# Four-layer decoder on one core: score and value matmuls of a batch issued together in the two 16-head cross-attention stages

## The reference

```
q = x_n @ w_q                  # 4 x 256 x (16 x 64)
k, v = context @ w_k, context @ w_v   # 4 x 512 x (16 x 64)
p = softmax(q k^T / 8)         # per head: 256 x 512
x = x + (p v) @ w_out + b_out
```

## Time and profile before

| | |
|---|---|
| runs shown | 2795.58, 2800.47, 2803.43 us |
| profiled execution | 2792.92 us, span 2791.1 us, mean granted PE clock 0.941 |
| PE busy | 2510.5 us, 90% of the span |
| PE weight loads | 1594.0 us, 57% |
| DVE busy | 1776.8 us, 64% |
| ACT busy | 1530.3 us, 55% |
| POOL busy | 1364.9 us, 49% |
| L918, scores matmuls | 768 instructions, 190.3 us |
| L945, flips of layer 0's cross stage | 512 instructions, median 273 ns |
| L968, value matmuls | 1280 instructions, 167.0 us |

### The profile page before, as it was taken

One profiled execution on the slowest core, in us unless ns is written; L12 is line 12 of the kernel. 1 busy time (PEld: TensorE's weight loads), 2 busy tenths in 40 slices (PEclk: granted clock), 3 DMA queues, 4 the chain that ended last, 5 costly groups with the idle time before them and its releaser, 6 DMA issues. The chain is left out here.

```text
span 2791.1 us, 57927 instructions
## 1 busy us (share of the span) xinstructions
PE 2510.5 (90%) x20585; PEld 1594.0 (57%) x20585; DVE 1776.8 (64%) x4074; ACT 1530.3 (55%) x4979; POOL 1364.9 (49%) x1981
## 2 busy tenths in 40 slices
PE   6899978988989988978559999789999999999997
PEld 3555544645655655646444555446666666666665
DVE  4566655545656755555554555478887888778884
ACT  2455544622756755633224555357667776777664
POOL 0344443400536642420003444388878878788873
PEclk8899998998998999999777999899999999999998
DMA  2000000000000010000010000101011011101000
GB/s 72 1 1 1 1 9 1 10 27 14 2 5 1 2 34 1 1 6 1 8 29 1 1 1 1 52 20 36 24 32 35 24 36 32 36 24 43 25 22 11
DMA packets 45711, 47.85 MB, mean 17 GB/s; under 512 B 11947, under 2 KB 31413, under 8 KB 45430
## 3 DMA queue, kind: packets, MB, share of 16 engines
q1 hardware_dynamic: 45430, 44.18, 5.7%
HBM read 31.05 MB, written 0.52 MB: 11 GB/s over the span
## 5 line engine op out<-in xcount | busy, mean ns | idle before, releaser
L1033 DVE TENSOR_REDUCE negmax<-scores 128x1 f32<-128x508 f32 (+4 forms) x512 | 212.5, 467 | 212.4 <-PE scores L918 181.1
L1013 POOL TENSOR_TENSOR l_xattn_probs<-l_xattn_probs,rowinv 128x512 f32<-128x512 f32 x128 | 130.4, 1040 | 421.1 <-DVE rowinv L1025 421.1
L2277 ACT ACTIVATE net_probs<-bank,net_negmax 128x96 f32<-128x96 f32 x768 | 251.6, 340 | 112.0 <-DVE net_negmax L2413 111.0
L1013 POOL TENSOR_TENSOR lora_probs<-lora_probs,rowinv 128x508 f32<-128x508 f32 (+1 forms) x256 | 149.6, 618 | 245.0 <-DVE rowinv L1025 245.0
L2331 POOL TENSOR_TENSOR net_rope<-net_rope,net_sin_parts 128x512 f32<-128x512 f32 x192 | 244.5, 1273 | 10.4 <-DVE net_sin_parts L2383 10.4
L2339 POOL TENSOR_TENSOR net_probs<-net_probs,net_inverse 128x384 f32<-128x384 f32 x192 | 158.8, 827 | 119.7 <-DVE net_inverse L2409 118.0
L2352 POOL TENSOR_TENSOR net_rope<-net_rope,net_head_inv 128x512 f32<-128x512 f32 x192 | 201.4, 1049 | 7.5 <-POOL net_head_inv L1882 0.9
L124 DVE COPY turned<-flip 128x512 f32<-128x512 f32 (+3 forms) x280 | 163.1, 583 | 65.2 <-PE flip L945 52.1
L739 DVE TENSOR_REDUCE negmax<-scores 128x2 f32<-128x256 f32 (+2 forms) x192 | 157.6, 822 | 64.0 <-PE scores L647 34.5
L918 PE MATMUL scores<-kT,qM 64*128 64x512 f32 (+2 forms) x768 | 190.3, 572 | 6.1 <-ACT kT L122 2.5
L986 ACT ACTIVATE lora_probs<-scores,negmax 128x508 f32<-128x508 f32 (+1 forms) x256 | 117.8, 472 | 138.4 <-DVE negmax L1033 137.6
(11 more groups left out here) (435 smaller groups left out, 6551.9 us busy)
## 6 DMA issues: line engine op xcount, KB each, us to landing
net_w_qkv<-in_L_ffn_Wqkv SPq DMA_DIRECT2D x12, 768.0 KB, 6.0
net_vals_between<-net_vals SPq DMA_DIRECT2D x48, 192.0 KB, 2.5
net_w_out<-in_L_ffn_Wo SPq DMA_DIRECT2D x6, 512.0 KB, 4.3
net_vals_between<-net_vals SPq DMA_DIRECT2D x48, 64.0 KB, 2.0
moe_w<-in_L_ffn_w13T SPq DMA_DIRECT2D x8, 256.0 KB, 2.7
net_w<-in_L_ffn_W SPq DMA_DIRECT2D x6, 341.0 KB
moe_w<-in_L_ffn_w2T SPq DMA_DIRECT2D x8, 128.0 KB, 2.4
ctx_tok<-in_ctx SPq DMA_DIRECT2D x1, 768.0 KB, 6.6
```

Of the source, the lines that this page charges most:

```text
L1013: last = nc.gpsimd.tensor_tensor(own, own, rowinv[:, u * tail + w:u * tail + w + 1].to_broadcast([P, k1 - k0]), ALU.mult)
L1033: last = nc.vector.tensor_reduce(negmax[:, u * tail + w:u * tail + w + 1], scores[:, 2 * qt + h, k0:k1], AX.X, ALU.max, negate=True)
L2277: last = nc.scalar.activation(prob_blocks(g)[:, w, :], score_blocks(g)[:, w // 2, w % 2, :], ACT.Exp, bias=maxima[:, g % 4, w:w + 1], accu ...
```

## The change

In the cross kind, TensorE's order within a pair of half steps changes; no instruction is added or left out, and the other engines' programs stay as they are.

- Even half step: S of query tile 0 and S of query tile 1, then O, the non-late fill, F and the late fill. No V.
- Odd half step: no S. F comes first, then the non-late fill (k), then V of part 0 and V of part 1 of batch (s - 5)/2, each after its own wait for the copies of the flips.

The second S waits, as before, for the second pair of exponentials of the batch before. For the causal kind, with one part, the order of the instructions is what it was; there only the order of waits ahead of V differs.

```diff
--- before.py
+++ after.py
@@ -900,28 +900,29 @@
                                 v.chunk.mm(proj[:, :], n).then_inc(in_filled.sem, 1)
                     def step(s, i, live):
-                        pair, g, qt = half_at(s, 0, live)
-                        if pair is not None:
-                            n, r = i + pair, 2 * g + qt
-                            if r % 4 == 0:
-
-                                wait_in(n, ("q", r // 4))
-                            if r % span == 0:
-
-                                wait_in(n, ("k", r // span))
-
-                            pe.wait_ge(exped.sem, exped.at(n, 4 * (g - 1) + 2 * qt + 2))
-                            nk, t = nk_of(qt), QT * g + qt
+                        pair, g, half = half_at(s, 0, live)
+                        if pair is not None and (half == 0 or not cross):
+                            n = i + pair
+                            if (2 * g + half) % 4 == 0:
+
+                                wait_in(n, ("q", g // 2))
+                            if (2 * g + half) % span == 0:
+
+                                wait_in(n, ("k", 2 * g // span))
                             k0 = g * (M if cross else N)
-                            for h in range(2):
-                                rows = pair_rows(h)
-                                last = nc.tensor.matmul(scores[:, 2 * qt + h, 0:nk], qM[rows, 0, t * P:(t + 1) * P], kT[rows, k0:k0 + nk],
-                                                        start=True, stop=cross)
-                                if cross:
-                                    last.then_inc(scored.sem, 1)
+                            for qt in range(QT) if cross else (half,):
+
+                                pe.wait_ge(exped.sem, exped.at(n, 4 * (g - 1) + 2 * qt + 2))
+                                nk, t = nk_of(qt), QT * g + qt
+                                for h in range(2):
+                                    rows = pair_rows(h)
+                                    last = nc.tensor.matmul(scores[:, 2 * qt + h, 0:nk], qM[rows, 0, t * P:(t + 1) * P], kT[rows, k0:k0 + nk],
+                                                            start=True, stop=cross)
+                                    if cross:
+                                        last.then_inc(scored.sem, 1)
                             if not cross:
                                 for h in range(2):
-                                    nc.tensor.matmul(scores[:, 2 * qt + h, nk - P:nk], ident16[:, :], masks16[:, CAUSAL, :],
+                                    nc.tensor.matmul(scores[:, 2 * half + h, nk - P:nk], ident16[:, :], masks16[:, CAUSAL, :],
                                                      start=False, stop=True).then_inc(scored.sem, 1)
                         for c in range(2):
                             pair = at_step(s, out_steps[c], live)
@@ -930,7 +931,8 @@
                                 pe.wait_ge(heads_moved.sem, heads_moved.at(n, 2 * c + 2))
                                 mm_tok(outT, w_o[:, bass.ds(n, 1), :].rearrange("p o d -> p (o d)"), 4 * c)(heads[:, :]).then_inc(out_filled.sem, 1)
-                        fill(s, i, live, False)
+                        if not cross or s % 2 == 0:
+                            fill(s, i, live, False)
                         for p, part in enumerate(parts):
                             pair, g = part_at(s, TURN, p, live)
                             if pair is not None:
@@ -946,21 +948,23 @@
                                                                        ident[:, :])
                                             c0 += P
                                     last.then_inc(flipped.sem, 1)
+                        if cross and s % 2 == 1:
+                            fill(s, i, live, False)
                         fill(s, i, live, True)
-                        for p, part in enumerate(parts):
-                            pair, g = part_at(s, VALUES, p, live)
-                            if pair is not None:
-                                n = i + pair
+                        pair, g = part_at(s, VALUES, NP_ - 1, live)
+                        if pair is not None:
+                            n = i + pair
+                            if 2 * g % span == 0:
+                                wait_in(n, ("v", 2 * g // span))
+
+                            pe.wait_ge(heads_moved.sem, heads_moved.at(n, g))
+
+                            pe.wait_ge(out_emptied.sem, out_emptied.at(n, g // 2))
+                            v0 = g * (KT if cross else QT)
+                            for p, part in enumerate(parts):
                                 for h in range(2):
                                     pe.wait_ge(moved[h].sem, moved[h].at(n, NP_ * g + p + 1))
-                                if p == 0:
-                                    if 2 * g % span == 0:
-                                        wait_in(n, ("v", 2 * g // span))
-
-                                    pe.wait_ge(heads_moved.sem, heads_moved.at(n, g))
-
-                                    pe.wait_ge(out_emptied.sem, out_emptied.at(n, g // 2))
-                                c0, v0 = 0, g * (KT if cross else QT)
+                                c0 = 0
                                 for j, q0 in part:
                                     w = (QT - q0) * P
                                     for h in range(2):
```

## The result

The changed kernel takes 2753.51 us in the median of four runs (2748.26 to 2757.32), the kernel before beside it 2798.02 (2793.9 to 2803.43): ratio 0.9838, 95% interval 0.9818 to 0.9859. A repetition in a later set gave 2748.58 against 2799.93, ratio 0.9819 (0.9792 to 0.9846). So the change is faster by 1.6 to 1.8%, 44.5 us in the first set where 31.8 were forecast, and the time lies 0.5 us under the range of 2754 to 2789. The profiled executions took 2792.92 and 2752.27 us, 40.6 us apart.

A forecast was written before the change was run, and what follows sets the result against it. TensorE's queue was taken as the bound: layer 3 14.1 + layer 0 14.1 + clock dip 1.6 + filling 2 = 31.8 us off the 2800.5 median, giving 2768.7 us; range 2754 to 2789 (own forecast 2761 to 2777, chance 0.57).

The forecast's parts named there:

- no new wait in the steady part: Cross stages: no idle time before the odd F, and S released by TensorE's own queue, not by ScalarE's k copy.
- The slacks: Margins before new waits: 0.4 to 0.5 us before the odd F, 0.2 before layer 3's next S; k just in time.
- rival 2: Layer 3: k's copy holds the next S, pairs take 8.99 us; 24 us less in all (2776), chance 0.10.
- rival 4: Odd F waits in every pair for copies of the even F: 35 us slower, 2835; over 2800 has chance 0.06.
- rival 5: Order changes, but all engines' couplings take the gain back: no difference, 2800 us, chance 0.06.
- rival 1: Grouping saves nothing, only the second S under the stall before v1 counts: 16 us less (2784), chance 0.14.
- The second S under the wait for q1: Half steps 2/3: second S fills idle time before v1; 1.13 us (layer 3) and 1.18 (layer 0) less, 7 times each.
- S+S 1.98 and V+V 1.96: Steady pairs: grouped blocks' times from start to start, in us; bounds 1.92 to 2.12 and 1.90 to 2.02.
- F 0.95 and k 1.06: Layer 3's odd half step: F 0.95 us as k awaits v's copy out of `proj`; k 1.06 before V.
- Rival 3: Each switch costs both ends, 0.2 us for each of three saved in 58 pairs: 51 us less (2750), chance 0.07.
- Filling and emptying, 2 us: Pipeline filling does S earlier and V later: 2 us gained, bounds -1 to +4.
- The dip of the earlier trace: Layer 0's stage: clock fell to 1.2 GHz after a 1.42 us stall, costing 1.6 us; expected gone.

The follow-up runs named there:

- the two splitting experiments: Changed kernel with one block put between two of a kind, same instructions and waits: split scores (median 15.0 us longer) and k between values (12.4 us longer).
- one wait: Changed kernel with the waits inside S+S and V+V drawn ahead of each group's first block: pairs 8.56 and 8.89 us, stages 4 to 6 us longer.
- scores wide: Kernel before with only S+S grouped in the even half step, V and k where they stood: median 37.8 us lower, stages 32.4 us shorter.
- values wide: Kernel before with only both V grouped in the odd half step, S and fills unchanged: ratio 0.9974, median 5.8 us lower, stages 11.2 us shorter.
- split scores: Changed kernel with O or the early fill between the two S: stages 12.1 us longer than the changed kernel's repetition, median 15.0 us longer.
- k between values: Changed kernel with k put between the two V of the odd half step: stages 11.5 us longer, median 12.4 us longer.
- q1 late: Changed kernel with q1 and v1 exchanged in half step 2: stages 6.2 us shorter than in the repetition, median 5.3 us longer.

## Why the prediction was wrong

- **Bound by TensorE's queue; the causal stage unchanged; no new wait in the steady part: right.** The slacks held to 0.1 us. Rivals 2, 4 and 5 are out, and rival 1 falls with the two splitting experiments.
- **The second S under the wait for q1: right.** v1 starts 3.93 and 4.48 us after S, as forecast; half steps 2/3 took 8.81 and 9.69 us (8.90 and 9.80).
- **The step that failed: the size of the grouping, S+S 1.98 and V+V 1.96.** Measured were 1.91 to 1.92, which is the lower bound given for S+S (1.92), and 1.87 to 1.88, which is under the one for V+V (1.90). V+V counts in all 58 steady pairs, S+S in the 44 in which the second S does not lie under the wait for q1: 0.09 x 58 + 0.07 x 44 = 8.3 us. The steady pairs lost 37.2 us besides the dip of the clock, where 28.2 were forecast, so the two sizes are 8.3 of the 9.0 missing; the rest is mostly layer 0's k, 1.17 where 1.20 was taken (29 x 0.03 = 0.9).
- **Where the two sizes came from.** V+V 1.96 is 1.01 + 0.95 from the one row with two V in a row, and that row holds an open wait; without it the same two V are 0.08 shorter (one wait). For S+S the forecast put 0.46 us between inner instructions. The changed kernel's weight loads of S start at 1512.73, 1513.27 and 1513.70, so the inner distance is 0.43. k's row had pointed to it, for 0.96 less the 0.53 of an outer one is 0.43 too; none of the rows shown gives 0.46.
- **F 0.95 and k 1.06 in the odd half step of layer 3: right.** Measured were 0.94 to 0.95 and 1.06.
- **What a change of block costs.** S takes 1.06 between other blocks and 0.96 in the mean beside its like, V 1.01 and 0.93 to 0.94. By pairs of half steps, one change less was worth 0.20 us for S and 0.15 for V (scores wide, values wide), and two changes more cost 0.35 and 0.17 (split scores, k between values): 0.09 to 0.20 us for a change. The rule of the Trainium skill that was cited (TensorEngine Tiling (Array Packing), Tiling Modes), that a change of the tiling mode drains TensorE, agrees with the trace for S and V, as the two splitting experiments show. Rival 3 is right in that blocks on both sides pay (O and F in split scores). Its 51 us are too many: S+S, V+V and v gained 0.21, 0.15 and 0.10 in an ordinary pair of layer 3, not 0.2 each, and it counted nothing for k, which lost 0.10.
- **Filling and emptying, 2 us: too small.** Filling, which is the time from the first S to the fifth half step's, gave 3.9 (19.3 to 17.0 us in layer 0 and 21.5 to 19.9 in layer 3; 2.6 in the repetition) and emptying 0.6. The dip of the earlier trace rows is gone, 1.6, as forecast.
- The parts add to 37.2 + 1.6 + 3.9 + 0.6 = 43.3 us in the stages, where 31.8 were forecast. The profiled executions lie 40.6 apart, because outside the stages the changed one was 2.8 us longer. That the medians lie 44.5 apart is within the 9 to 10 us over which either kernel's runs spread, and so is the half microsecond by which the time lies under the range. The 11.5 us missing in the stages are not.

## What to carry to other kernels

Where TensorE's queue is the bound, group blocks of one shape. Each change between 64-row, 64-column and full blocks cost about 0.1 to 0.2 us here, and waits already met inside a group were free. Before a row is taken as the price of a block, look whether a wait inside it was still open: the one row with two V in a row was 0.08 us too long for that. When two fills share one PSUM bank, put a block about as long as the copy between them; without it the same grouping lost more than it won. And judge a gain of under 10 us by the time of the stage that was edited, because the clock's low stretches elsewhere move the total by as much.

## What the hardware showed

- The low stretch at the start of layer 0's feed-forward part lasted 17 to 41 us in kernels whose instructions there are the same. The time outside the edited stages went with it: 2168.6 to 2171.1 us with 41.0 us, 2158.8 to 2164.7 with 17.1 to 27.3. In q1 late TensorE was busy 36.21 of 41 us at 1.2 GHz before the clock rose. What picks the length stays open; that a kernel that comes there 5 us earlier can meet a longer one is shown by q1 late.
- q1 late lost this time in all of its five runs (2752.05 to 2755.35 us, mean granted clock 0.937 to 0.939), while four of the five of the repetition beside it had 0.943 or 0.944 and one 0.940 (2758.30 us). So averaging over more runs of one kernel need not remove it.
